# VectorE's wait for the pair in front, in the last pooling pass of a recommender kernel

## What is computed

```python
mask = (sequence_ids != 0)[..., None]                      # (1024 users, 200 ids)
seq_emb = where(mask, item_embeddings[clip(sequence_ids - 1, 0)], 0.0)
pooled = seq_emb.sum(axis=1) / maximum(mask.sum(axis=1), 1)
user_rep = pooled @ W_rec.T + b_rec                        # 512 wide
retrieved = item_embeddings[retrieved_indices].mean(axis=1)    # 50 rows a user
gate = sigmoid(concat([user_rep, retrieved], axis=1) @ gate_W.T + gate_b)
fused = gate * user_rep + (1.0 - gate) * retrieved
logits = fused @ proj_W.T + proj_b                         # (1024, 12500)
```

## Time and profile before

| | |
|---|---|
| median of 3 runs | 2170.16 us |
| lowest and highest | 2169.76 and 2172.5 us |
| profiled execution, its time | 2164.81 us |
| its span (first to last instruction) | 2163.1 us |
| mean granted clock of TensorE | 0.972 |
| busy: TensorE, VectorE, ScalarE, GpSimd | 96%, 74%, 38%, 52% |

### The profile page before, as it was taken

The page is one execution under the profiler, slowest core; times in us unless marked ns, Lnnn a source line. Parts: engine busy times, 40 slices in busy tenths (PEclk is TensorE's granted clock), DMA queues, the critical chain, the costliest instruction groups (busy, mean ns, idle before and its releaser), DMA issues.

```text
span 2163.1 us, 32100 instructions
## 1 busy us (share of the span) xinstructions
PE 2073.7 (96%) x12762; PEld 1069.4 (49%) x12762; DVE 1600.2 (74%) x1837; ACT 817.9 (38%) x1009; POOL 1123.6 (52%) x830
## 2 busy tenths in 40 slices
PE   4669999999999999999999999999999999999999
PEld 4555555555555554444444444444444444444444
DVE  8999999888888786544577777687878865555554
ACT  5866677445444555435212112232211222212111
POOL 5674562788678865656366666656667600000000
PEclk7559999999999999999999999999999999999999
DMA  8999997999899987879589998877899975666765
GB/s 299 334 236 290 285 330 252 308 251 256 239 277 244 253 287 261 312 244 326 178 282 329 315 309 298 298 247 261 319 312 346 372 237 172 205 216 235 234 216 188
DMA packets 222050, 586.82 MB, mean 271 GB/s; under 512 B 21840, under 2 KB 121040, under 8 KB 218576
## 3 DMA queue, kind: packets, MB, share of 16 engines
q1 hardware_dynamic: 91424, 264.21, 36.0%
q0 software_dynamic: 77632, 218.16, 35.9%
q10 hardware_dynamic: 52848, 102.41, 12.6%
HBM read 448.21 MB, written 136.48 MB: 270 GB/s over the span
## 4 chain that ended last, share of the span: by engine, by line
PE 79%; DVE 8%; POOL 6%; ACT 3%; issue 2%; DVEq 1%; DMA 1%; another core or an unknown queue 0%; ACTq 0%; POOLq 0%
PE pooled_ps L1328 35%; PE pooled_ps L1221 22%; PE count_ps L1328 9%; PE count_ps L1203 6%; PE count_ps L1233 6%; POOL gathered L577 3%; DVE row_hots L676 2%; POOL gathered L555 2%; ACT counts L986 2%; DVE keys L678 2%; ACT counts L980 1%; DVE recip L693 0%; DVE gathered L721 0%; DMA gathered<-emb,ret_rows 0%; DVE ring L683 0%
## 5 line engine op out<-in xcount | busy, mean ns | idle before, releaser
L1221 PE MATMUL pooled_ps<-mid,ring 128*128 128x512 f16 x3136 | 727.3, 380 | 4.9 <-ACT mid L1004 2.6
L555 POOL DMA_INDIRECT gathered<-emb,ret_rows x460 | 561.3, 1220 | 310.6 <-DVE gathered L721 150.1
L1221 PEld LDWEIGHTS pooled_ps<-mid,ring 128*128 128x128 f16 x3136 | 292.7, 98 | 312.1 <-issue 9.5
L577 POOL DMA_INDIRECT gathered<-emb,ret_rows x184 | 348.8, 1896 | 129.6 <-ACT ring L994 58.1
L1328 PE MATMUL pooled_ps<-counts,keys 128*128 128x500 f16 x1920 | 415.4, 374 | 0.0
L1328 PE MATMUL pooled_ps<-counts,mid 128*128 128x500 f16 x1920 | 413.2, 374 | 0.6 <-DVE counts L767 0.6
L950 DVE SCALAR_TENSOR_TENSOR ring<-pooled_ps,out_scale,counts 128x500 f32<-128x500 f32 x320 | 234.5, 736 | 231.2 <-PE pooled_ps L1328 208.7
L676 DVE TENSOR_TENSOR row_hots<-pair_columns,keys 128x2048 f16<-128x2048 f16 x256 | 313.2, 1223 | 68.7 <-PE count_ps L1203 54.5
L1109 ACT ACTIVATE counts<-counts,strip_scale 128x2000 f16<-128x2000 f32 x75 | 147.0, 1960 | 513.2 <-PE pooled_ps L1328 296.5
L1203 PE MATMUL count_ps<-keys,row_hots 128*128 128x98 f16 x4096 | 281.2, 225 | 59.8 <-DVE keys L678 42.9
L1203 PEld LDWEIGHTS count_ps<-keys,row_hots 128*128 128x128 f16 x4096 | 251.1, 107 | 139.0 <-DVE keys L678 56.3
(11 more groups left out here) (134 smaller groups left out, 1121.9 us busy)
## 6 DMA issues: line engine op xcount, KB each, us to landing
logits<-ring ACTq DMA_DIRECT2D x99, 1000.0 KB
ring<-emb_parts SPq DMA_DIRECT2D x147, 512.0 KB
counts<-proj_t SPq DMA_DIRECT2D x75, 1000.0 KB
counts<-emb SPq DMA_DIRECT2D x14, 1792.0 KB, 12.2
emb_parts<-ring SPq DMA_DIRECT2D x49, 512.0 KB, 7.7
mid<-emb SPq DMA_DIRECT2D x46, 512.0 KB
counts<-proj_b SPq DMA_DIRECT2D x75, 250.0 KB
gathered<-emb,ret_rows POOLq DMA_INDIRECT x660
```

Source lines behind the costliest of these rows:

```text
L555: pool.indirect_dma_start(slots[group][:, a], None, source, column(block, r * SLOT + a))\
L577: pool.indirect_dma_start(to, None, source, column(block, n), compute_op=ALU.add).then_inc(landed, 16)
L1221: last = pe.matmul(pooled_ps[:, m], ring_v[:, p % RING, c, part, m * P:(m + 1) * P], cvt[:, p % CVT, c], start=(i == 0 and c == 0 and part ...
```

## The change

In VectorE's loop over the steps of the last pass the wait for the pair in front goes. All other waits of VectorE stay, and no instruction is added, dropped or moved.

```diff
                     if g == 0 and 0 < i < NP - 3:
                         split_low(i + 3)
-                    if g == NG - 1 and i > 0:
-                        wait_pair(dve, g * NP + i - 1)
                     if g == NG - 1:
 
                         dense_parts(i, PASS)
```

## The result

The change made the kernel slower by 1%: 2192.47 us (four runs, 2187.55 to 2202.52) against 2170.94 us for the kernel before on the same chip (four runs, 2169.76 to 2172.5), a ratio of 1.0101 [1.0084, 1.0118]. The prediction, 2170.2 us and no change, was wrong, and the time lies above its range. The profiled execution took 2193.81 us, its span 2192.1 us against 2163.1 us before: 29.0 us to be found.

The account below looks back on a forecast made before the run. TensorE was taken as the bound, busy 96% of the span; all four parts came to 0 us, so the forecast was the median, 2170.2 us, range 2165.5 to 2175.0 us.

Parts of the forecast that it names:

- What bounds the kernel: Last pooling pass: TensorE busy 226.86 of 230.00 us, idle 3.1 us; the removed wait lies on VectorE, with 109 us slack.
- Part 3: Earlier additions free buffers, so GpSimd issues gathers sooner in the last pass, but enters the logits stage unchanged: 0 us.
- the 13.21 us: VectorE's idle time before its addition at 940.69 us, releaser not named; read as waiting for the pair's signal.
- Part 1: 47 waits fewer on VectorE in the last pass: at most 53.7 us of its idle time goes, worth 0 by itself.
- Part 2: Dense work VectorE hands to TensorE in the last pass, four hand-overs: stays or is covered, sum 0 us at TensorE.
- the mix: VectorE's multiplication at step 26 (L737): to start at about 949.0 instead of 951.66 us, the 2.7 us lost later.
- GpSimd's standstill at the end of the pass: Sign: GpSimd's wait for a next-stage addition, 27.26 us before, should grow by what GpSimd gained earlier.
- rival 3: Faster: GpSimd's gather lead outlives the pass, removing TensorE's 3.6 us wait for retrieved rows and 3.1 us: 2163.5 us; chance 0.04.
- Part 4: End of the pass: last paced addition and moves of pooled sums slightly earlier, TensorE's cover 6.8 us; value 0.
- Rival 1: VectorE's dense hand-overs wait for ScalarE, which waits for pairs, so the trace hardly changes: 2170.2 us; chance 0.17.
- Rival 2: Slower: gathers brought forward delay ScalarE's load of pool sums, TensorE standing up to 6.4 us: 2176.6 us; chance 0.07.
- The rule on turns between queues: DMA engines alternate between queues packet by packet, so gathers can't wholly precede the pool-sums load; would leave rival 2 near 2170.

Follow-up runs that it names:

- g0_after: The changed kernel, unaltered, run again beside the kernel before (2162.28 us) on a quiet chip: 2162.97 us, ratio 1.0004.
- group 2: Second set of runs, on a chip where the kernel before took 2172.35 us; the changed kernel, repeated there, took 2190.74 us, ratio 1.0089.
- c_gathers_wait: The changed kernel, but GpSimd waits before last-pass refills for the pair VectorE's freeing addition used to wait for: 2173.37 us, ratio 1.0014.
- h1_two_breaks: The changed kernel with GpSimd waiting twice in the last pass, behind additions 67 and 81, until its gathers landed: 2176.76 us, ratio 1.0001.
- h2_direct: The changed kernel with plain transfers of 128 neighbouring rows replacing the last pass's gathers, so wrong rows are retrieved: 2167.18 us, ratio 0.9982.
- c_after: The changed kernel, unaltered, repeated on a loud chip beside the kernel before (2172.35 us): 2190.74 us, ratio 1.0089.

## Why the prediction was wrong

**What bounds the kernel.** That TensorE is the bound was right. The step that failed is in this part and in Part 3: I read 3.1 us of idle time as a stretch in which nothing is wrong, and did not ask what its 2.2 us without a releaser and the 13.21 us of "remote" were a sign of. I took the 13.21 us as an ordinary wait for a pair. It was one, but for a signal that came late, and the place where it stood, at the end of a run of gathers, was the hint.

**Part 1**, 47 waits less, worth 0 by itself: held. VectorE did run ahead; its two groups of additions over the pass of the kernel after have 7.3 + 3.6 us of idle time in place of 43.0 + 3.6:

```profile
L721 DVE TENSOR_TENSOR gathered<-gathered 128x1024 f32<-128x1024 f32 x48 | 58.8, 1226 | 7.3 <-DMA gathered<-emb,ret_rows 1.7 <-issue 1.7
L721 DVE TENSOR_TENSOR gathered<-gathered,mid 128x1024 f32<-128x1024 f32 x9 | 11.0, 1227 | 3.6 <-DMA mid<-emb,ret_rows 2.8 <-issue 0.2
```

**Part 2**, hand-overs to TensorE, 0 us: held, for TensorE has no wait in the pass for anything VectorE makes. By g0_after, where nothing else disturbs, the mix starts 942.25 - 861.66 = 80.6 us after the first L796, where the earlier trace rows give 85.4 us; predicted was 949.0 - 866.28 = 82.7 us. Of the 2.1 us that the forecast is off, 1.7 are the two gaps of TensorE in between (1.03 and 0.66 us), which that chip doesn't have.

**Part 3**, additions and gathers earlier, 0 us: this is the term that failed. The gathers did come earlier, as it says. Its value was not 0 but some 26 us in the pass on a loud chip (29.0 us of the span, less the 4.6 behind the pass, plus the 1.9 that this execution was ahead when it began; by the medians the whole change costs 21.5 us there and 18.4 us in group 2). I had counted only what a gather's earlier issue does for its consumer, and nothing for what an unbroken run does to others on the way. That an earlier engine removes pauses, and that the pauses were worth something, is what I missed. On a quiet chip the term is 0, as said: 1.0004 in g0_after, whose later wait for the retrieved rows is 3.5 us against 3.6. One sign failed on both chips: GpSimd's standstill at the end of the pass was to grow beyond 27.26 us by what it had gained, and is 26.86 us after and 26.10 us in g0_after. The lead was gone before the pass ended, which also speaks against rival 3.

**Part 4**, the end of the pass, 0 us: not contradicted. The last move is 24.4 us late for the pass's sake, and the trace shows no wait of TensorE for L704.

**Rival 1**, the wait implied by others, fell: the additions lost their idle time, which now stands ahead of the dense hand-overs (23.19 us ahead of the mix after). **Rival 2**, slower because the load of the pool sums is delayed, had the right sign and the right suspect, gathers brought forward, with the wrong mechanism: no wait for L796 in the pass. It was priced as a delay of one load, up to 6.4 us, and so at 2176.6 us. The rule on turns between queues that stood beside it was not put to the test. **Rival 3**, faster, fell too.

**The chances.** With 0.87 for no change I had the answer of the one quiet chip on which the change ran, and not that of the first result and of group 2. I had one profile, of one chip, and built the range from its own idle time.

**What stays open.** What in GpSimd's issue of gathers holds TensorE up: c_gathers_wait, h1_two_breaks and h2_direct say that it goes, or nearly, when the issue pauses or is done another way, no more. Why the same issue does no harm in other runs of 30 to 173 us on a loud chip isn't known either. Whether a pair wait only at steps 11 to 17 would do on a loud chip was not measured, as both of its repeats met quiet ones. Why chips differ isn't known, and executions differ too: on the loud chip of group 2 one of the ten of the kernel after took 2172.92 us, as the kernel before. No profile of the kernel before on a quiet chip is on record, so its gaps can't be compared there. All times come from executions that were recorded in the same way; whether the recording has a part in it can't be told from them. And no kernel beat the kernel before, beyond h2_direct's 0.2%, which leaves the gathering of the right rows out.

## What to carry to other kernels

A wait that looks idle can be the brake of a loop: before taking it away, follow what it frees (here additions, buffers, gathers) to the engine that then runs without a pause, and ask what happened to the bound engine at the ends of that engine's longest runs before. In the trace of the kernel before, small gaps of the bound engine without a releaser and "remote" waits on its consumers, which stand together at such ends, are a warning and deserve a rival of their own, with a price that may be several times their size (here 2.2 us before, 15.1 us after). And a difference of 1% that one chip shows should be tried on a second one, in both directions.

## What the hardware showed that was not expected

- TensorE does 42 matmuls in 30 us in place of 137 while no row names a wait of its for operands, in the late part of a run of 35 transfers issued by GpSimd in 45.9 us. The Trainium skill, page "SBUF — State Buffer", section "Who interferes with whom", says that TensorE and ScalarE never wait on anyone, the one contention being that for the port pair of VectorE and GpSimd. No run here shows a port or a memory as the cause, but these runs do show TensorE being held up while GpSimd issues; where the sentence is read as "GpSimd's work can't slow TensorE", the measurement decides against it.
- Its signals reach other engines 20.8 us after the recorded end of the matmuls in the kernel after (ScalarE's 19.40 us of "remote" at 894.59 us), and 27.0 us in c_after (27.09 us of "remote" at 902.88 us).
- The same issue of gathers goes unnoticed elsewhere in the same execution: 35 transfers in 59.7 us with the queues' share at 1.01, and TensorE busy for 60.00 of 60.00 us.
- Chips differ: the kernel before takes 2162.3 to 2162.9 us in three groups of runs and 2170.9 to 2178.6 us in the four others, the first result among them; the change costs 1.0004 on one of the former and 1.0089 and 1.0101 on the latter.
- Two pauses of GpSimd of about 4 us, well placed, cost nothing (1.0004 on a quiet chip) and come out even with the kernel before on a loud one (1.0001); breaks at every sixth addition cost 7 to 9 us on a quiet one.
- After its gaps TensorE's granted clock fell to 0.50 (1.2 GHz) for 20.5 us, which lengthened a loss that it did not begin.
